# Pass 1 of the next expert unit's first four heads inside each unit's section, and weights issued by ScalarE

## What is computed

```python
    x = x + _L0_attn_ref(_layernorm(x, axis=-1), ...)
    x = x + _L0_ffn_ref(_layernorm(x, axis=-1), ...)
    x = x + _L1_attn_ref(_layernorm(x, axis=-1), ...)
    x = x + _L1_ffn_ref(_layernorm(x, axis=-1), ...)
# _L0_ffn_ref, for each of 4 experts e:
        member = (top2 == e).any(-1)
        order = jnp.argsort((~member).astype(jnp.int32), axis=-1, stable=True)
        xg = jnp.take_along_axis(x, order[..., None], axis=1)
        q = (xg @ wq[e] + bq[e]).reshape(b, s, h, hd)
        ...
        att = jnp.einsum('bqhd,bkhd->bhqk', q, k) * sm_scale
        att = jnp.where(validg[:, None, None, :], att, -1000000000.0)
        att = jax.nn.softmax(att, axis=-1)
        y = jnp.einsum('bhqk,bkhd->bqhd', att, v).reshape(b, s, d)
        y = y @ wo[e] + bo[e]
        out = out.at[bidx, order].add(wg[..., None] * y)
```

## Time and profile before

| | us |
|---|---|
| median of 3 runs | 4642.21 (4641.92 to 4647.13) |
| the profiled execution | 4639.23 |
| its span | 4637.4 |
| busy in the span: PE, DVE, ACT, POOL | 3578.4, 2441.7, 2102.3, 926.9 |
| first layer's attention, to the first unit's start | 914.7 |
| sixteen units | 914.7 to about 3300 |

### The profile page before, as it was taken

How to read it: one execution, slowest core, us unless ns; L and a number is a source line. 1 busy time by engine, 2 the same in 40 slices (tenths; PEclk the granted TensorE clock), 3 DMA queues, 4 the chain that set the end, 5 groups by cost and what they waited for, 6 DMA issues and landing times.

```text
span 4637.4 us, 57466 instructions
## 1 busy us (share of the span) xinstructions
PE 3578.4 (77%) x20509; PEld 1607.6 (35%) x20510; DVE 2441.7 (53%) x5520; ACT 2102.3 (45%) x4546; POOL 926.9 (20%) x686
## 2 busy tenths in 40 slices
PE   3998988586697877797767978579458878787896
PEld 1443433322232323322233233323223434344574
DVE  3765656361273622645235543246266788876623
ACT  1664655354356444373533735237225535453121
POOL 1142322310210102001021000110232414010274
PEclk8998999788899888898878989789779989899898
DMA  5453443411331214312033121340242323122388
GB/s 140 152 160 115 140 132 122 116 47 56 101 78 31 62 44 115 76 29 70 25 110 88 42 57 30 93 106 22 74 128 76 105 64 103 46 72 96 82 207 222
DMA packets 326588, 421.37 MB, mean 91 GB/s; under 512 B 43996, under 2 KB 283044, under 8 KB 316678
## 3 DMA queue, kind: packets, MB, share of 16 engines
q1 hardware_dynamic: 302228, 373.50, 28.3%
q0 software_dynamic: 18432, 35.67, 3.3%
q10 hardware_dynamic: 5248, 4.79, 0.3%
HBM read 240.32 MB, written 164.04 MB: 87 GB/s over the span
## 4 chain that ended last, share of the span: by engine, by line
PE 49%; DVE 24%; issue 7%; ACT 6%; DMA 5%; SPq 3%; POOL 2%; PEldq 2%; ACTq 1%; another core or an unknown queue 1%; PEld 0%; POOLq 0%; DVEq 0%
PE PSUM L728 12%; PE PSUM L691 9%; PE PSUM L706 9%; DVE M L949 8%; PE PSUM L637 6%; DVE M L952 5%; ACT P L889 3%; DVE PSUM L955 2%; PE PSUM L750 2%; PE PSUM L673 2%; DVE best L1282 1%; DVE XR L1285 1%; PE PSUM L736 1%; DMA ye_d<-P,lists 1%; PE PSUM L569 1%
## 5 line engine op out<-in xcount | busy, mean ns | idle before, releaser
L889 ACT ACTIVATE P<-PSUM 128x512 f32<-128x512 f32 (+2 forms) x3520 | 1558.3, 504 | 867.5 <-PE PSUM L706 543.6
L691 PE MATMUL PSUM<-KS,QS 99*128 99x512 bf16 (+3 forms) x3520 | 943.0, 359 | 491.4 <-SPq L1841 262.8
L949 DVE TENSOR_REDUCE M<-PSUM 128x1 f32<-128x896 f32 (+3 forms) x960 | 938.4, 1023 | 649.9 <-PE PSUM L691 645.7
L706 PE MATMUL PSUM<-QS,KS 101*128 101x512 bf16 (+2 forms) x3520 | 1069.7, 348 | 124.0 <-ACT P L889 73.9
L728 PE MATMUL PSUM<-P,VA 128*17 128x512 f32 (+3 forms) x7040 | 793.5, 522 | 10.4 <-ACT P L889 10.4
L952 DVE TENSOR_REDUCE M<-PSUM 128x1 f32<-128x640 f32 (+6 forms) x704 | 584.2, 830 | 193.6 <-PE PSUM L691 175.7
L706 PEld LDWEIGHTS PSUM<-QS,KS 101*128 101x128 bf16 x3520 | 328.6, 100 | 977.2 <-ACT P L889 592.6
L691 PEld LDWEIGHTS PSUM<-KS,QS 99*128 99x128 bf16 x3520 | 298.7, 102 | 950.5 <-SPq L1841 269.5
L620 POOL TENSOR_TENSOR QF<-QF,PH 128x1024 f32<-128x1024 f32 (+1 forms) x98 | 174.5, 1780 | 2235.7 <-ACT PH L853 2196.4
L955 DVE CUSTOM_DVE_ANT_0 PSUM<-PSUM,mask 128x128 f32<-128x128 f32 x1024 | 283.8, 300 | 199.6 <-PE PSUM L691 173.0
L1017 DVE RECIPROCAL RD<-PSUM 128x16 f32<-128x16 f32 (+2 forms) x160 | 38.0, 238 | 615.8 <-PE PSUM L736 615.5
(11 more groups left out here) (189 smaller groups left out, 3324.5 us busy)
## 6 DMA issues: line engine op xcount, KB each, us to landing
qk_d<-PH SPq DMA_DIRECT2D x192, 256.0 KB
xg_d<-GX SPq DMA_DIRECT2D x19, 1152.0 KB, 11.3
yg_d<-GX SPq DMA_DIRECT2D x17, 1152.0 KB
QS<-qk_d SPq DMA_DIRECT2D x48, 384.0 KB, 5.0
KS<-qk_d SPq DMA_DIRECT2D x48, 384.0 KB, 5.9
XF<-xg_d SPq DMA_DIRECT2D x18, 1024.0 KB
VA<-n_L_ffn_expert_gate_up_w SPq DMA_DIRECT2D x64, 256.0 KB, 5.8
qk_d<-PH SPq DMA_DIRECT2D x108, 128.0 KB
```

The costliest lines, as they stand in the source:

```text
L691: mm = e.matmul(slot_heads(s, hb)[:, x, a:b], QS[0:KA, g, h + x, 128 * qt:128 * qt + 128], KS[0:KA, g, h + x, a:b], start=True, stop=True)
L706: mm = e.matmul(s[:, 0:q1 - q0], KS[0:KB, g, j, 128 * kt:128 * kt + 128], QS[0:KB, g, j, q0:q1], start=True, stop=not diag, skip_group_che ...
L889: e.activation(P[:, m % NP, 0:q1 - q0], s[:, 0:q1 - q0], ACT.Exp, scale=ly.scale).then_inc(S["act_p"], 1)
L949: e.tensor_reduce(m[:, 0, qt, h:h + hb], v[:, :, 0:kn], AX.X, ALU.max).then_inc(S["dve_a"], 1)
```

## The change

Pass 1 of group 0 leaves the head of each section and stands in the section of the unit before, over the end of its pass 2 (`first_pass(coming, 2, 0, t0, long)`); for the first unit it stands at the end of the first layer. It is done for 4 or 8 blocks, as the next unit is prepared. Pass 2 of group 0 can begin right after the value projections. The times in `unit_order` are written anew, for all sizes alike. The loads of heads 0 to 3, the mask and group 0's row DMA are waited for inside the section; the semaphores of heads 4 to 7 are still carried. `mt` for the next unit waits until the rows of groups 1 to 3 have landed, and its row DMA until pass 2 of the old group 0 is done. `nx` and `wo` move from SP's queue to ScalarE's, where they stand first in the section. Where the next unit is of 4 blocks, the second half of its projections has columns of its own in QF and PH (`half`), and no longer waits for the first half's split and store. The body of `nx` and `wo` is unchanged; the functions `next_weights` and `output_weights` hold it.

```diff
+    def half(self, i, g2):
+
+        return 512 * g2 if self.layer.name == "moe" and self.layer.of(i).n == 512 else 0
+
...
+def first_pass(layer, i, g, t0, long):
+
+    ev = []
+    tiles = [(qt, h) for qt in range(layer.nt) for h in range(0, 4, layer.heads(qt))]
+    cost = [75 + 1.04 * layer.keys(qt) * layer.heads(qt) for qt, h in tiles]
+    done = 0
+    for x, task in zip(cost, tiles):
+        ev.append((t0 + 0.82 * long * done / sum(cost), ("s1", i, g) + task))
+        done += x
+    if layer.causal:
+        ev.append((t0 + 0.822 * long, ("mc", i, g)))
+    ev.append((t0 + 0.825 * long, ("mh", i, g)))
+    ev.append((t0 + 0.826 * long, ("ml", i, g)))
+    turn = 0.88 if layer.causal else 0.83
+    ev.append((t0 + turn * long, ("mt", i, g)))
+    ev.append((t0 + (turn + 0.001) * long, ("mr", i, g)))
+    return ev
+
+
 def attention_steps(layer, i, first, second):
 
 
     ev = []
     for g in range(4):
-        t0, long = first[g]
-        tiles = [(qt, h) for qt in range(layer.nt) for h in range(0, 4, layer.heads(qt))]
-        cost = [75 + 1.04 * layer.keys(qt) * layer.heads(qt) for qt, h in tiles]
-        done = 0
-        for x, task in zip(cost, tiles):
-            ev.append((t0 + 0.82 * long * done / sum(cost), ("s1", i, g) + task))
-            done += x
-        if layer.causal:
-            ev.append((t0 + 0.822 * long, ("mc", i, g)))
-        ev.append((t0 + 0.825 * long, ("mh", i, g)))
-        ev.append((t0 + 0.826 * long, ("ml", i, g)))
-        turn = 0.88 if layer.causal else 0.83
-        ev.append((t0 + turn * long, ("mt", i, g)))
-        ev.append((t0 + (turn + 0.001) * long, ("mr", i, g)))
+        if first[g]:
+            ev += first_pass(layer, i, g, *first[g])
         t0, long = second[g]
         groups = [(qc, kt) for qc in range(layer.nch) for kt in layer.key_tiles(qc)]
         width = [140 + layer.queries(*x)[1] - layer.queries(*x)[0] for x in groups]
...
+        ev += first_pass(layer.of(B), B, 0, 20.3, 0.6)
...
-    step, alone, rows = 0.84 * nt * nt, 0.6 * nt * nt, 8.0
-    first = [(0.0, alone / 0.82)] + [(alone + step * g, step) for g in range(3)]
-    second = []
-    for g in range(4):
-        t = first[g][0] + 0.82 * first[g][1] + rows
-        second.append((max(t, second[-1][0] + step) if second else t, step))
+
+    nt, coming, ev = layer.nt, layer.next, []
+    step, small = max(0.84 * nt * nt, 3.4), nt <= 4
+    first = [None] + [(step * g, step) for g in range(3)]
+    second = [(0.4 * len(layer.pairs()) + 0.3, step)]
+    for g in range(1, 4):
+        t = first[g][0] + 0.82 * first[g][1] + 8.0
+        second.append((max(t, second[-1][0] + step), step))
+    over = [t + 1.06 * step for t, _ in second]
     ev += attention_steps(layer, 1, first, second)
-    ev += [(-1.0 + 0.1 * w + 0.05 * g, ("ql", 1, w, 2 + g)) for w in range(2) for g in range(2)] + [(-0.7, ("mk", 1, 1)), (-0.5, ("wo", 1))]
-    ev += [(1.0 + 2.0 * k, ("vp", 1, c, h)) for k, (c, h) in enumerate(layer.pairs())]
-    ev += [(first[1][0] + 2.0, ("bv", 1)), (first[1][0] + 4.0, ("bb", 1))]
-    end = second[1][0] + step
+    ev += [(-1.0 + 0.1 * w + 0.05 * g, ("ql", 1, w, 2 + g)) for w in range(2) for g in range(2)]
+    ev += [(-0.7, ("mk", 1, 1)), (-0.6, ("nx", 2)), (-0.5, ("wo", 1))]
+    ev += [(0.05 + 0.4 * k, ("vp", 1, c, h)) for k, (c, h) in enumerate(layer.pairs())]
+    ev += [(second[1][0] + 1.0, ("bv", 1)), (second[1][0] + 2.0, ("bb", 1))]
+    x = 0.4 * len(layer.pairs()) + 0.1
+    ev.append((x, ("nv", 2)))
+    ev += [(x + 1.5 * c + 0.75 * k, ("xt", 2, c, k)) for c in range(coming.nch) for k in range(2)]
+    ev.append((x + 3.0, ("nr", 3)))
+    back = x
+    for g2 in range(2):
+        y = x + 3.5 if g2 == 0 else x + 15.0 if small else max(x + 23.5, second[1][0])
+        for w in range(2):
+            for c in range(coming.nch):
+                ev.append((y, ("qp", 2, w, g2, c)))
+                y += 2.5 if g2 == 0 or small else 6.0
+            ev += [(y - 1.0, ("spl", 2, w, g2)), (y + 6.0, ("qs", 2, w, g2))]
+        if g2 == 0:
+            back = y + 7.0
+            ev += [(max(over[g], back) + 0.1 * w + 0.3 * g, ("ql", 2, w, g)) for w in range(2) for g in range(2)]
+            ev.append((max(over[1], back) + 0.2, ("mk", 2, 0)))
+    t0 = max(first[3][0] + 0.83 * step, max(over[1], back) + 2.0)
+    long = max((second[3][0] + 0.8 * step - t0) / 0.82, 0.4 * coming.nt ** 2)
+    ev += first_pass(coming, 2, 0, t0, long)
     for c in range(layer.nch):
         t = max(t for t, task in ev if task == ("nt", 1, 3, c))
         ev += [(t + 0.5 + 0.3 * k, ("yt", 1, c, k)) for k in range(2)]
         ev += [(t + 2.0 + 0.5 * h, ("op", 1, c, h)) for h in range(2) if layer.pair(c, h)]
-    ev.append((t + 2.8, ("yo", 1)))
-    x = 1.0 + 2.0 * len(layer.pairs())
-    ev += [(-0.6, ("nx", 2)), (x, ("nv", 2))]
-    ev += [(x + 1.5 * c + 0.75 * k, ("xt", 2, c, k)) for c in range(layer.next.nch) for k in range(2)]
-    ev.append((x + 3.0, ("nr", 3)))
-    x += 3.5
-    for g2 in range(2):
-        y = x if g2 == 0 else x + 13.0 if step < 20.0 else max(x + 20.0, second[1][0])
-        for w in range(2):
-            for c in range(layer.next.nch):
-                ev.append((y, ("qp", 2, w, g2, c)))
-                y += 2.5 if g2 == 0 or step < 20.0 else 6.0
-            ev += [(y - 1.0, ("spl", 2, w, g2)), (y + 6.0, ("qs", 2, w, g2))]
-    ev += [(max(end - step * (1 - g), x + 18.0) + 0.1 * w + 0.2 * g, ("ql", 2, w, g)) for w in range(2) for g in range(2)]
-    ev.append((max(end, x + 18.0) + 0.3, ("mk", 2, 0)))
+    ev.append((max(t for t, task in ev) + 1.0, ("yo", 1)))
...
-            name, n = O.split(i, wi, g2)[0], O.layer.of(i).n
-            f, hi, mid, lo = QF[:, wi, 0:n], PH[:, wi, 0, 0:n], PH[:, wi, 1, 0:n], PH[:, wi, 2, 0:n]
+            name, a = O.split(i, wi, g2)[0], O.half(i, g2)
+            b = a + O.layer.of(i).n
+            f, hi, mid, lo = QF[:, wi, a:b], PH[:, wi, 0, a:b], PH[:, wi, 1, a:b], PH[:, wi, 2, a:b]
             done = O.at(name, *task)
             if O.layer.name == "l1":
                 w.wait_ge("act_x", "rh", i, wi, g2)
             else:
                 w.wait_ge("act_a", "qp", i, wi, g2, O.layer.of(i).nch - 1)
-            if g2 == 1:
+            if g2 == 1 and a == 0:
                 w.wait_ge(f"qst{wi}0", "qs", i, wi, 0)
-            else:
+            elif g2 == 0:
                 w.wait_ge(f"qst{wi}1", "qs", i - 1, wi, 1)
...
-                        if moe and g < 2:
-                            w.carried(f"ahead_ld{wi}{g}", 48)
+                        if moe and i == 1 and g == 1:
+                            w.carried(f"ahead_ld{wi}", 48)
                         else:
                             w.wait_ge(f"qld{wi}{g}", "ql", i, wi, g)
-                    if moe and g < 2:
-                        w.carried("ahead_mask", 16)
-                    if moe and g >= 2:
+                    if O.ahead(i):
+                        w.wait_ge("mask0", "mk", i, 0)
+                    elif moe and g >= 2:
                         w.wait_ge("mask1", "mk", i, 1)
...
-                    if g2 == 1:
+                    if g2 == 1 and O.half(i, g2) == 0:
...
-                    x, a = s[:, 0:m], 512 * c
+                    x, a = s[:, 0:m], 512 * c + O.half(i, g2)
...
+                    if moe and O.ahead(i):
+                        for x in range(1, 4):
+                            w.wait_ge(f"mrow{x}", "mr", i - 1, x)
                     w.wait_ge("pe_a", *task)
                     e.activation(ly.row_slot(MR, g), flat(s)[0:8, 0:n], ACT.Copy).then_inc(S["act_a"], 1)
                 elif kind == "mr" and moe:
                     g = task[2]
                     w.wait_ge("act_a", "mt", i, g)
+                    if O.ahead(i):
+                        w.wait_ge("pe_s", "s2", i - 1, g, O.layer.nch - 1, O.layer.nt - 1, 3)
                     row_of_maxima(e, ly, g)
+                elif kind == "nx" and moe:
+                    next_weights(e, v)
+                elif kind == "wo":
+                    output_weights(e, v)
...
```

69 lines of the change are left out of this document (35 added, 34 removed).

## The result

The changed kernel takes 4608.46 us (median of 4, 4603.83 to 4611.48), the kernel before 4643.86 us (median of 4, 4641.92 to 4647.13). The ratio is 0.9922, 95% interval 0.9905 to 0.9939. It is 0.8% faster, by 35 us instead of the 86 that were forecast, and lies inside the range, 52 us above the predicted time. The profiled execution has a span of 4608.3 us against 4637.4.

What follows compares the result with a forecast made beforehand. No single engine was taken to set the time. Large sections 208 plus size 2 20, minus size 3 100, minus end of first layer 42, gave 86 us gained: 4639.2 - 86 + 3 = 4556 us, range 4510 to 4645.

Steps and rivals of the forecast that it cites:

- The price of a tile: Large sections: a pass-1 tile beside exponentials costs 0.18 us at 896 elements, 0.21 at 1024, against a microsecond alone.
- 4 x 36.2: Size-7 section: four groups at the old last group's time, 144.8 us, within 192.1 to the last exponential; 21.7 gained each.
- three quotients: Tile prices from group differences: first against last and third against last at size 7, first against last at size 6.
- The first rival: TensorE really is as full as its rows say, 93% in the fullest groups: 4643 us, no change; chance 0.14.
- last group over 46: Sign in a size-7 section: a last group over 46 us, against about 41 forecast, means occupancy was real.
- low end by occupancy: Large sections with TensorE at 93%: 8 us gained instead of 22 at size 7, 121 together instead of 208.
- Tiles from +64 at 1.5 us each: Size 3, rival that small sections eat the gain: +52 us each, 4664; chance 0.14 together with no effect.
- Size 6: Four large sections, next unit of 4 blocks: last exponential at +149.1 us, 28 gained each, 112 in all.
- Size 3: Four small sections that take the next unit's 32 tiles: 25 us longer each, 100 in all; bounds +15 and +36.
- End of the first layer: First unit's first pass stands alone there, once: 42 us lost, bounds 33 and 48, start at about 954.
- Size 2: Four small sections: 5 us gained each, 20 in all, by earlier weights and new halves of PH and QF.
- Weights on ScalarE: Seven weight DMAs hold ScalarE some 4 us, costed at nothing; may give an earlier first projection in small sections.

Runs made afterwards that it cites:

- experiment 9: Changed kernel with next unit's tiles spread, turn behind them, first 512 queries' output behind the last group, and small sections' projections first: ratio 0.9837 to the kernel before.
- Experiment 2: Kernel before, leaving out all but the last pass-1 tile of the third head group in units over four blocks: 4561.76 us beside 4610.56.
- experiments 5 and 6: Changed kernel, large sections: turn (maxima split, transposed, copied, sent as row) late, behind the last exponential, ratio 0.9877; tiles spread as well, 0.9876.
- experiment 12: Changed kernel with one half of PH and QF used again for both head halves in units of 4 blocks: ratio 0.9915 to the kernel before.
- experiment 11: Changed kernel with the next unit's and the output weights issued by SyncE again, not ScalarE: ratio 1.0054 to the kernel before.

## Why the forecast was off, step by step

**The price of a tile was mis-sized and the turn had no term, and the base that both came from is why.** The step "first against last group at size 7: (41.8 - 36.2) / 29 = 0.19" compared a group with pass 1, and so with its turn, to one without the turn but with 5.9 us of output. The forecast had no term for the turn: as the last group had none, the fourth term of 4 x 36.2 left it out there, and in the other three groups it was paid for by output that they don't hold. With the measured parts (bare group 30.3, turn 4.2, output 5.9; that the turn costs as much in the first three groups was not measured) the groups of before give (41.8 - 34.5) / 29 = 0.25 for the first and (39.7 - 34.5) / 21 = 0.25 for the third, and (47.8 - 34.5 - 28 x 0.25) / 4 = 1.6 for a projection. The next unit's tiles, when spread, cost about what was forecast: (41.6 - 36.2) / 25 = 0.22, and (36.1 - 30.3) / 25 = 0.23 in experiment 9. The same sum with these, for the size-7 section at 2477.9: 9.7 + 4 x 34.5 + 5.9 + 84 x 0.25 + 32 x 0.22 + 12.8 + 3.2 = 197.6. Forecast 192.1, measured 205.0. The dearer tiles make up 5 of the 12.9 missing (84 x 0.07, less 0.9 that the base had too much). For the last size-7 section (8 tiles, 4 projections) it gives 9.5 + 138 + 5.9 + 21 + 1.8 + 6.4 + 2.1 = 184.7, against 184.9 measured and 179.6 forecast. Seen group by group it is the last one that failed: 36.2 + 25 x 0.21 = 41.5 forecast and 48.6 measured, of which 4.2 are the turn and 2.8 the packing; with both undone it takes 41.6. Four times base plus turn is 138, and with the output 143.9, while the forecast had 144.8: there the two errors cancelled by luck, and in the tile price they did not.

**The agreement of three quotients proved nothing.** 0.19, 0.17 and 0.19 all rested on the same kind of last group. Experiment 2 gives 0.17 to 0.30, with a mean near 0.25, and 0.25 and 0.27 at size 7 at full clock.

**Packing was not foreseen.** 32 tiles of 1024 elements were laid at 1.4 units each ahead of the last fifth of the group. 2.8 us up to the last exponential come from spacing alone (experiments 5 and 6).

**Nor was the clock.** In the section at 2477.9 both first groups were granted 0.97 and take 52.2 and 51.2 us. With 1.00 the same groups take 50.3 (section at 1892.3) and 50.0 (spread kernel):

```profile
1903.00:1953.30 50.30, 46.42 (x263) 16.32 (x262) 30.25 (x32) 35.16 (x72) 10.62 (x6) 1.00 0.38 97
...
2521.50:2571.50 50.00, 45.98 (x259) 15.97 (x258) 31.42 (x36) 34.09 (x68) 10.59 (x6) 1.00 0.24 61
```

That is 3.1 us more. About 1.5 of the 12.9 stay unexplained; the second group takes 50.0 at full clock against 48 forecast, and its bias row and four projections were not tried alone.

**The first rival** (TensorE as full as its rows say) had set the test "last group over 46", and it came true at 48.6. But not by its mechanism: 4.2 of the excess were the turn, the packed stretch with TensorE at 95% gets through 12 of ScalarE's instructions and the spread one at 100% through 16, and experiment 9 has the same tiles in a 36.1 us group with TensorE at 97% (without the output and the turn). The Trainium skill's warning against matmul occupancy as a measure ("Perfetto Trace Analysis", Identifying the Most-Contended Engine) is borne out by that pair of rows, 88% busy in 48.6 us and 97% in 36.1. The share of weight loads, which it wants instead, is 31% in both rows and tells them apart no better.

**Slips in the recorded sums.** The low end by occupancy is (195.6 - 28 x 0.46 + 32 x 0.53) / 0.93 = 215 and not 213, so 6 us instead of 8 a section. Tiles from +64 at 1.5 us each, by the prediction's own steps, end with the section 48 us longer and not 52, which gives 4648 and not 4664. And a start near 954 is 39 us behind 914.7, where 42 was taken. None of them moves the 4556 by more than 3 us.

**Size 6** came out as forecast, 27 us against 28, and in part by luck. It has 8 tiles of the next unit, and its last group has room: the late turn saved only 0.9 us there. But the same step was wrong here too: a tile cost 0.26 to 0.30 in experiment 2, not 0.19, which would be 5 us and more for 72 tiles, and the section shown ends its last exponential only 1.7 us later than forecast. What gives the rest back was not found.

**Size 3**: the relay was put right (first tile at +52.4 for +51, last at +94.2). Each section is 29 us longer and not 25. Most of that stands in the silence behind the row DMA: 14.6 us from its issue's end to the next start, where 11.4 were carried over from before. **End of the first layer**: 33 for 42, the same term with the other sign, as only 6.5 us pass between the issue's end at 941.2 and the start. **Size 2**: 20 for 20, but not for the reason given. The halves of PH and QF have no share in it that can be measured (experiment 12), and ScalarE's weights 1.3 us a section (experiment 11); what gives the other 3.6 was not tried.

**Weights on ScalarE** were costed at nothing, and their gain was sought in the small sections. They are a condition of the whole: without them, the new place of the first projection costs some 49 us over all sections (4 x 4.6 + 3 x 3.4 + 9.0 + 4 x 1.6 + 4 x 1.3), more than the whole gain of the change, as the ratios say too, 0.9922 and 1.0054. The forecast placed those projections without asking when their bias lands. The Trainium skill ("DMA: Bandwidth & Descriptors", Issuing engines are not separate DMA queues) says that a further issuing engine saves only the sequencers' time; the rows agree that no transfer got faster, as the key bias took 11.7 us to land instead of 8.6; but the time saved, 8 us of SP's queue ahead of it, is as long as the transfer itself here and not small beside it.

## What to carry to other kernels

A price got by subtracting two stages is good only if the lists of work in both have been written down side by side, with the small serial steps in them, not the engine's largest item alone; take the base from a stage in which one thing is missing, or make one. Work that is hidden beside a pipeline has a price that depends on its spacing: the first dozen of tiles in this group cost 0.1 us each, and the thirteen after them 0.6. Before a difference of one or two us between two stages is read as a price, compare the granted clock in both. When an operation is moved forward, ask for each of its operands, the smallest too, when it is issued and when it lands.
